# Moving output products ahead of waits, and adding matmuls whose result nobody reads, in a two-attention layer with experts

## What is computed

```python
x = x + layernorm(attn(layernorm(x)))                # 16 heads of 16, rotary positions,
                                                     # causal window of 250 keys
x = x + layernorm(ffn(layernorm(x)))

def ffn(src):
    sa  = attention2(src) @ Wo                       # 16 heads, all 512 keys, compressed k and v
    x   = rmsnorm(src + sa, norm1_w)                 # the "expert source"
    shared = swiglu(x @ W_shared_in) @ W_shared_out
    w   = top2 of 8 gated experts (2 groups)         # from x @ Wg_gate, x @ We_gate
    h   = swiglu(x @ W1_shared)
    routed = sum_e (h @ W2_experts[e]) * w[:, e]
    return rmsnorm(x + shared + routed, norm2_w)
```

## Time and profile before

| | |
|---|---|
| time, median of 3 executions | 2315.79 us (2305.55 to 2317.77) |
| the profiled execution: its own time | 2326.53 us |
| its span, first to last instruction | 2324.5 us |
| granted TensorE clock over the span | 0.881 of full speed |
| TensorE matmul busy | 2059.2 us, 89% of the span |
| VectorE busy | 1385.1 us, 60% |
| ScalarE, GpSimd busy | 831.0 us (36%), 342.1 us (15%) |
| DMA | 104.69 MB, 44 GB/s of HBM over the span |

### The profile page before, as it was taken

One profiled execution on the slowest core, in us unless ns is written; L12 is line 12 of the kernel. 1 busy time (PEld: TensorE's weight loads), 2 busy tenths in 40 slices (PEclk: granted clock), 3 DMA queues, 4 the chain that ended last, 5 costly groups with the idle time before them and its releaser, 6 DMA issues.

```text
span 2324.5 us, 31756 instructions
## 1 busy us (share of the span) xinstructions
PE 2059.2 (89%) x9200; PEld 1081.4 (47%) x9200; DVE 1385.1 (60%) x4293; ACT 831.0 (36%) x1714; POOL 342.1 (15%) x647
## 2 busy tenths in 40 slices
PE   6868799898999989999898988989889999999986
PEld 4343445535364443635445353453635445354445
DVE  6456455755757465674667556476575745747454
ACT  2423424262433424334242532326233252423410
POOL 3322113101320003100031011210112001210000
PEclk7566889998998987989899898799899897889998
DMA  4003002010030101201021000211002110020212
GB/s 165 2 28 136 1 2 92 37 38 10 9 130 1 48 1 66 72 2 48 1 83 56 31 17 1 83 55 38 11 2 100 37 48 1 7 90 34 74 55 91
DMA packets 23089, 104.69 MB, mean 45 GB/s; under 512 B 3312, under 2 KB 14192, under 8 KB 18288
## 3 DMA queue, kind: packets, MB, share of 16 engines
q1 hardware_dynamic: 21168, 89.81, 10.7%
q0 software_dynamic: 1728, 12.58, 1.4%
HBM read 84.56 MB, written 16.78 MB: 44 GB/s over the span
## 4 chain that ended last, share of the span: by engine, by line
PE 68%; DVE 20%; issue 7%; ACT 3%; DMA 1%; DVEq 0%; POOL 0%; SPq 0%; POOLq 0%; ACTq 0%
PE fb L734 13%; PE fb L712 11%; PE sm L646 10%; PE ot L686 10%; PE st L672 5%; PE st L615 3%; DVE negmax L1013 2%; DVE acc L1201 2%; DVE stats L927 2%; PE st L631 2%; PE dn L615 2%; PE dn L654 2%; PE dn L698 2%; PE sm L672 2%; DVE sm L1010 1%
## 5 line engine op out<-in xcount | busy, mean ns | idle before, releaser
L536 ACT ACTIVATE probs<-st 128x512 f32<-128x512 f32 (+3 forms) x832 | 404.7, 506 | 486.1 <-PE st L672 438.6
L646 PE MATMUL sm<-k_t,q_t 48*128 48x512 f32 (+3 forms) x928 | 385.8, 496 | 102.6 <-DVE negmax L1010 49.3
L734 PE MATMUL fb<-w_r,h_r 128*128 128x512 f32 x1536 | 444.9, 426 | 13.2 <-DVE acc L1201 13.2
L1013 DVE TENSOR_REDUCE negmax<-sm 128x1 f32<-128x512 f32 x464 | 302.1, 686 | 136.2 <-PE sm L646 135.5
L646 PEld LDWEIGHTS sm<-k_t,q_t 48*128 48x128 f32 x928 | 170.8, 213 | 439.4 <-DVE negmax L1010 211.3
L672 PE MATMUL st<-q_t,k_t 64*128 64x512 f32 (+3 forms) x832 | 352.2, 478 | 14.3 <-ACT probs L536 12.1
L734 PEld LDWEIGHTS fb<-w_r,h_r 128*128 128x128 f32 x1536 | 279.8, 195 | 126.4 <-issue 60.1
L712 PE MATMUL fb<-xn_t,wup_s 128*128 128x512 f32 x512 | 321.5, 723 | 6.5 <-DVE h_s L1186 4.1
L1010 DVE CUSTOM_DVE_ANT_0 sm<-sm,mask_qk 128x384 f32<-128x384 f32 (+2 forms) x464 | 213.3, 467 | 190.9 <-PE sm L646 188.5
L686 PE MATMUL ot<-probs,v_s 128*32 128x512 f32 (+3 forms) x2048 | 276.3, 563 | 2.9 <-POOL probs L439 1.8
L672 PEld LDWEIGHTS st<-q_t,k_t 64*128 64x128 f32 x832 | 153.2, 203 | 135.1 <-ACT probs L536 87.1
(11 more groups left out here) (166 smaller groups left out, 2464.1 us busy)
## 6 DMA issues: line engine op xcount, KB each, us to landing
w_r<-w_parts SPq DMA_DIRECT2D x32, 2048.0 KB, 7.8
w_parts<-w_r POOLq DMA_DIRECT2D x4, 2048.0 KB, 8.9
x_s<-in_L_attn_query SPq DMA_DIRECT2D x8, 512.0 KB, 4.6
h_s<-in_L_ffn_W_experts POOLq DMA_DIRECT2D x8, 512.0 KB, 6.3
q_t<-rot_b SPq DMA_DIRECT2D x256, 4.0 KB
x_kept<-o_s SPq DMA_DIRECT2D x8, 512.0 KB, 3.0
xa<-x_kept SPq DMA_DIRECT2D x8, 512.0 KB, 3.5
out<-acc SPq DMA_DIRECT2D x8, 512.0 KB, 11.4
```

The lines of the kernel that those rows point to most:

```text
L536: nc.scalar.activation(probs[:, n % PSLOTS, 0:hi - lo], score_bank(m)[:, 0:hi - lo], ACT.Exp, scale=float(D) ** -0.5).then_inc(s_ex, 1)
L646: mm(max_bank(w)[:, 0:hi - lo], q_t[r:r + MROW, b, t * P:(t + 1) * P], k_t[r:r + MROW, b, lo:hi], start=True, stop=True).then_inc(s_sm, 1)
L734: last = mm(fb[q % 2][:, :], h_r[:, h, m, rows], w2_r[:, k % 2, w, m, :], start=(m == 0 and n == 0), stop=(m == NH - 1 and n == 2))
L1013: return v.tensor_reduce(negmax[:, g % 2, n // GH, c:c + 1], max_bank(g * UNITS + n)[:, 0:hi - lo], AX.X, ALU.max, negate=True).then_inc(s ...
```

## The change

Four things change.

1. **TensorE, order.** In the first heads product 17 stands ahead of the projections (`OUT_ROWS[0]`, right after the row transposes) instead of beside tile 0. In the second heads product 7 moves to the middle, ahead of the wait for the second source (`OUT_ROWS[1]`), and product 8 from tile 3 to tile 2. VectorE reads them where it read them before.
2. **TensorE, unread products.** `keep_warm(dst, n)` issues n plain float32 matmuls (128 x 128 by 256 columns) into a bank whose content nobody reads. They stand in both attentions of batch 0 (every step of the lead, every second step after), 16 in the middle of batch 0, four steps of the lead of each later first attention, seven steps of the lead of each later second attention, one after each transpose of the second source, and 8 + 4 in the last expert stage.
3. **Steps beside the first attention.** The source's transposes go from m = -26 to -28, the logits from -21 to -24, and the first 16 hidden matmuls from the steps -18 to -1 to the steps -21 to 2; the four others of the first head group move by up to two steps.
4. **VectorE.** 18 of the 22 steps of `expert_source` run ahead of the first heads, the four weightings in pairs beside tiles 0 and 1. In both heads `copy_stacks` comes ahead of `beside`.

```diff
-ROWS_FROM, LOGITS_AT = 2 - LEAD, 7 - LEAD
+ROWS_FROM, LOGITS_AT = -LEAD, 4 - LEAD
-QUIET = [g * UNITS + n for g in range(NGR) for n in (2, 5, 8, 12)]
+QUIET = [g * UNITS + n for g in range(NGR) for n in ((2, 5, 8, 12) if g else (4, 6, 9, 12))]
-HIDDEN_AT = spread(8 * NH - len(QUIET), 10 - LEAD, -1) + QUIET
+HIDDEN_AT = spread(8 * NH - len(QUIET), 7 - LEAD, 2) + QUIET
 OUT_HEADS = {0: ((17,), (), (18,), (19,), ()), 1: ((), (7,), (), (8,), ())}
+OUT_ROWS = {0: (17,), 1: (7,)}
+OUT_MADE = {0: ((), (), (18,), (19,), ()), 1: ((), (), (8,), (), ())}
+WARM_LEAD = {0: [m - LEAD for m in (1, 2, 3, 5)], 1: [m - LEAD for m in range(2, LEAD, 4)]}
+WARM_ROWS, WARM_FIRST_ROWS, WARM_LAST = 1, 16, 8
-SOURCE_STEPS = 8
+SOURCE_FIRST, SOURCE_STEPS = 18, 2
...
 # TensorE: attention(), after max_rows
+                    if f is None and (m < 0 or m % 2 == 0):
+                        keep_warm(fb[0], 1)
+                    if f is not None and m in WARM_LEAD[a]:
+                        keep_warm((dn, ot)[a], 1)
...
+            def keep_warm(dst, times):
+                for _ in range(times):
+                    mm(dst[:, 0:E], ident[:, :], wout_t[:, 0, :], start=True, stop=True)
...
 # TensorE: heads()
-                        for q in OUT_HEADS[a][t]:
+                        for q in OUT_MADE[a][t]:
                             out_rows(f, q)
...
 # TensorE: batch()
                 transpose_rows(xa, pair, s_tp)
+                if e is not None:
+                    for q in OUT_ROWS[0]:
+                        out_rows(e, q)
                 pe.wait_ge(s_tc, i * N_TC + NC)
...
                 if f is not None:
-                    for q in OUT_FIRST:
+                    for q in (*OUT_FIRST, *OUT_ROWS[1]):
                         out_rows(f, q)
+                else:
+                    keep_warm(fb[0], WARM_FIRST_ROWS)
                 pe.wait_ge(s_xn, i + 1)
                 transpose_rows(xn, pair, s_tp)
+                keep_warm(fb[0] if f is None else st[1], WARM_ROWS)
...
 # TensorE: after the last batch
+            keep_warm(dn, WARM_LAST)
             experts_rows(B - 1, B - 2)
+            keep_warm(dn, WARM_LAST // 2)
             gate_logits(B - 1)
...
 # VectorE: heads()
-                    beside(t)
                     if t >= 1:
                         copy_stacks(i, a, t - 1)
+                    beside(t)
...
 # VectorE: batch()
+                for _ in range(SOURCE_FIRST):
+                    next(source, None)
                 heads(i, 0, beside_first)
...
 # VectorE: after the last batch
-                for _ in range(SOURCE_STEPS):
+                for _ in range(STEPS_AT_LAST):
```

## The result

The changed kernel takes 2372.89 us (median of 4 runs, 2359.95 to 2386.99), the kernel before, on the same chip, 2316.78 us (4 runs). The ratio is 1.026, 95% interval 1.0212 to 1.0308: slower by 56 us. The forecast was 2277 us, with 2235 to 2355 as its range; the time lies outside it, on the other side of no change, and 8 us above the far end of case 4.

A forecast was written before the change was run, and what follows sets the result against it. TensorE, busy 89% of the span and partly at a low clock, was taken as the bound. Terms -16 + 14 + 6 + 13 - 6 - 18 - 29 - 3 = -39 us, applied to the median 2315.8, gave 2277 us, range 2235 to 2355.

The forecast's parts named there:

- case 4: Unread products run slower at the low clock, in batch 0 and first leads: 2343 us, up to 2365; chance 0.35.
- Batch 0: 120 unread products in its attentions: +26 us work, -32 from clock, net -6; bounds -27 and +71.
- the slope of -0.25: In batch 0, each of 129 us at the low clock that comes up saves 0.25 us: -32 us.
- later steps: In case 4, batch 0's steps after the leads give back about 11 us by a high clock.
- the good case: Batch 0's attentions with unread products at the high clock: net -6 us.
- Products 7 and 8: Moved in middle and second heads: +2.0 us a batch, +14 in seven; bounds 0 and +3.07 x 7 = +21.
- The second leads: Seven unread products each, batches 1 to 7: +13 us work, -18 as low time falls from 75 to 25 us.
- Steps beside the first attention: Hidden matmuls spread over 24 steps instead of 18, same work: 0 us, bounds +-7.
- the low stretches late in the first attentions: Sign that the forecast is wrong if these, in batch 5 but not 2, come out otherwise: 15 us each.
- The clock of the first leads: Four unread products bring up half of each 20 us low stretch, batches 1 to 7: -29 us, bounds 0 and -58.
- First heads: Early stack copies remove TensorE's wait: -2.5 us in batches 2 to 7, -1 in batch 1, -16 in all.
- Last stage: Last expert stage: unread products cost +1 us, less low clock gives -4, net -3.

The follow-up runs named there:

- e2: The kernel before plus only the 120 unread products in batch 0's two attentions: 2367.77 us, ratio 1.0201.
- e5: e2 plus 12 unread products back to back ahead of each of batch 0's two leads: 2314.79 us, ratio 1.0031 to the kernel before.
- e10: The kernel before with only products 7 and 8 moved, to the middle and ahead of the second heads' last projection: 2369.20 us, ratio 1.019.
- e1: The changed kernel without the 120 unread products in batch 0's attentions: 2296.46 us, ratio 0.9928 to the kernel before.
- e4: e1 with products 7 and 8 back in their old places in the second heads: 2249.80 us, ratio 0.9748 to the kernel before.
- e9: The kernel before with 18 early source steps, product 17 ahead of the first projection, and stack copies first in both heads: 2316.67 us, ratio 1.0022.
- e11: e4 without the four unread products in each first lead of batches 1 to 7: 2257.47 us, ratio 0.9744 to the kernel before.
- e12: e11 plus 12 unread products back to back ahead of each of batch 0's leads, none inside: 2262.18 us, ratio 0.9795 to the kernel before.
- e7: e6 plus the seven unread products in each second lead of batches 1 to 7: 2262.24 us, ratio 0.9776 to the kernel before.
- e8: The kernel before with only the steps beside the first attention moved: 2274.84 us, ratio 0.9843.
- e3: The changed kernel with every unread product left out, the moves kept: 2316.94 us, ratio 1.0022 to the kernel before.
- e6: The changed kernel without any unread product and with products 7 and 8 back in the second heads: 2297.28 us, ratio 0.9856 to the kernel before.

## Why the prediction was wrong

**Batch 0: the step that failed.** The forecast: "At the high level 54 us, less the 13.2 and 15.1 us in which TensorE has no matmul = +26. In return its 129 low us come up". Batch 0's low clock did not come up under the added work. It measured +76.8 us against -6, and that is 83 of the 96 us by which 2277 missed. What the step took for granted is that TensorE without a wait has the high clock; the lead is busy for 47.77 of 47.80 us, at 0.52. e2 shows that this part alone does it, e5 that the low clock is the cause: with the clock kept at 1.00 batch 0 is 60 us shorter, with the same 120 products and 24 more. The forecast's own bound at the low level was +71, and it was set aside for the slope of -0.25.

Case 4 named this mechanism and its sign ("batch 0's lead at 0.50 and near 40 us") and gave it 0.35; it sized it at +25 for batch 0. (Its far end is 2361 us by its own terms, 2343 and the 18 of the second leads, not 2365.) Two of its terms were short. A product was priced at 0.45 us (0.83 low) from output projections that stand back to back. Those of e5's burst do take 0.45; but one between two max scores takes 0.63, and 1.15 at the low level. With that, 28 x 1.15 - 4.9 = 27 us for the first lead, where 28.2 was measured. And the "later steps" that were to give back 11 us gave none: the rest of the first attention went from 59.8 to 77.6 us, of the second from 64.3 to 71.7, with 32 products in each.

**Clock gain against cost.** The forecast for the good case, -6, was wrong too. e5 has the clock at 1.00 in all of both attentions and they take 13.8 us more than before, plus 24 products: batch 0 lasts 262.0 us against 244.8. The price 0.63 instead of 0.45 is most of it (120 x 0.18 = 22 us).

**Products 7 and 8.** Forecast +2.0 us a batch, measured 3.8 in middle and heads (19.5 + 7.4 over seven). The term's upper bound, 3.07, left out the second step, product 8: ahead of the last projection it no longer covers the copies of the stacks, and a wait of 1.18 us stands there. What no term had is the clock. Heads that end in stacks alone leave TensorE at the low level in some batches, and the lead behind them then takes 34 to 38 us instead of 25 to 27 (e10, and e1 against e4). By stages that is 28 of e10's 54 us in batches 1 to 7.

**The second leads.** Forecast +13 - 18 = -5, measured +30.7, for that reason. The seven unread products cost 2.5 us a lead where the clock is 1.00 throughout (27.8 us in e1, 25.3 in e10; the forecast had 1.9) and don't lift a clock that is low when the lead begins: 26 us low in 38.2 (rows of batch 3). They may shorten a low stretch that begins within it: with VectorE's new order in the heads and without them the second leads have 105 us low (e9), with them 34 (e4), 44 (e11), 41 (e12) and 70 (e7); but e9 also lacks the moved steps, so this is a sign, not a proof.

**Steps beside the first attention.** Forecast "same work: 0", measured -36 us. The work is the same, but it stands in other places: transposes and logits earlier fill waits for VectorE, 18 us. The other half would have to be the clock (60 us less at the low level in e8), and how much of that is the steps' work stays open. The error is a term set to nothing because no work was added or taken away. The forecast had named the low stretches late in the first attentions as a thing that could spoil it, 15 us each; behind the leads there were 96 us low before and 34 after.

**The clock of the first leads.** Forecast -29 from four unread products, less 6 for their work; e11 against e4 gives 0, give or take 17 us by the two intervals. The first leads did become 30 us shorter in all (282.4 to 252.3), but by e8 (252.4) the steps did that. Some 14 us of it is no gain: two hidden matmuls of each lead now stand behind it (147 us of hidden matmuls in the seven leads before, 134 in e8).

**First heads.** Forecast -16, measured -18 in e9, where the "issue" ahead of TensorE's first work stays as the forecast had it: right. The -22 of the changed kernel is partly luck. There the "issue" of 10.3 us is gone, which no term had, and 6.3 us of waits for VectorE's first reading have come. The forecast laid the source steps into the 4.77 us that VectorE idles in the earlier trace rows; but VectorE stands idle for 3.2 to 4.1 us of its own at that place in batches 3 to 6 and begins them late. Against e2, which has neither this order nor the "issue", the first heads are 9.5 us shorter (196.7 to 187.2). That the gain then didn't reach the total in e9 is once more the clock of the second leads.

**Last stage.** Forecast -3, measured -4: right.

**The mean clock.** It rose from 0.881 to 0.898 in a kernel that became 2.6% slower, and e5, with 0.925, the highest of all, is at 1.003. Unread products raise the clock over time that they themselves take.

So the sum had the right sign for batches 1 to 7 (-17 against -30) by luck: an unforeseen gain of the moved steps and unforeseen losses of the second leads met. The version that the runs point to is e4 or e11: the heads' order, the moved steps and the second leads' unread products, without batch 0's products and without the move of 7 and 8. It takes 2250 to 2257 us, 2.5% under the kernel before and 5% under the change.

## What to carry to other kernels

Filler work for the clock has to be priced at the low level, singly as it will stand, and against the waits that it really fills; it can hold a high clock, but where the clock is low, or falls at the stretch's start, single pieces may not lift it and then cost near double. Before moving a wide matmul out of a narrow stretch, look at the stage behind it: the level at which that stage begins is worth more than the move. And a change with five parts wants five runs: here two parts were worth 1.6 and 0.9%, and two others ate them.

## What the hardware showed that was not expected

- TensorE at the low clock with no idle time, 47.77 us busy of 47.80, and no rise (e2 the same); 12 products in a row ahead of the same work, and no fall through the 85 us of the attention (e5). In both kernels the clock was at 1.00 when this began: what differs is whether it falls.
- An unread product (two records of 256 columns) takes 0.45 us in a burst, 0.63 us between two max scores at the high level, 1.15 at the low.
- The "issue" of 1.70 to 2.25 us ahead of the first projection, in five of the six later batches before (10.3 us in all), is absent from e2, whose only difference is 120 more products ahead of the loop. Its first heads are 12.6 us shorter. The batch in e2 that answers to the earlier trace rows, and the same place in e9, where no unread product is in the program:

```profile
1153.35 1.98 PE L615 MATMUL dn<-win_t,xn_t 128*128 128x512 f32 x4 [0.82 <-ACT xn_t L472]
```

```profile
1094.61 2.98 PE L741 MATMUL fb<-w_r,h_r 128*128 128x512 f32 x12 [1.93 <-issue]
```

TensorE's wait is there in every profiled kernel without unread products (before, e3, e6, e8, e9, e10) and in none with them (after, e1, e2, e4, e5, e7, e11, e12). The forecast let it stand, whatever was put in front of it. The Trainium skill, page "Runtime: NRT & Kernel Launch", section "Instruction fetch mechanics", says that instructions are fetched in blocks and that a taken branch to one that isn't there stalls; that the added instructions move the loop's start within such a block would fit this, but no run here tests it.
- VectorE has such a wait too, and it doesn't go with the unread products: in all nine kernels that make the source steps ahead of the heads (after, e1, e3, e4, e6, e7, e9, e11, e12) it stands in "issue" for 3.1 to 4.5 us before them, in batches 3 to 6 and not in 2 and 7. In the six of these in which TensorE's own wait is gone, TensorE waits 0.7 to 2.5 us in the same batches for VectorE's reading of the first tile. Of the time won by the one, the other takes a part back.
